# Last part of a decoder: the sums of the wide norm made on the activation engine, and the matrix engine a slot ahead

## The reference, cut to what matters

```python
h = layernorm(x, ln1_g, ln1_b)
h = bitlinear(h, w1, b1)                  # 256 -> 1024
h = jax.nn.gelu(h, approximate=False)
h = layernorm(h, ln2_g, ln2_b)            # over 1024 columns: "the wide norm"
h = bitlinear(h, w2, b2)                  # 1024 -> 256
x = _layernorm(x + h, axis=-1)
# bitlinear: x to integers in -128..127 by 127 / max|x| of the token, w to -1, 0, 1,
# the product, and both scales put back; layernorm: (x - mean) * rsqrt(var + 1e-5) * g + b
```

## Time and profile before

| | us |
|---|---|
| median of 3 runs | 2312.98 (2312.34 to 2318.16) |
| profiled execution | 2315.36 |
| its span | 2313.6 |
| last stage, from the first issue of a transfer to the end of the span | 2008.3 to 2313.6 |
| slot of the last stage (29 slots from the third `h` at 2032.46 to the last at 2291.71) | 8.94 |
| mean granted clock of TensorE over the span, as a share of full speed | 0.843 |

### The profile page before, as it was taken

How to read it: one execution, slowest core, us unless ns; L and a number is a source line. 1 busy time by engine, 2 the same in 40 slices (tenths; PEclk the granted TensorE clock), 3 DMA queues, 4 the chain that set the end, 5 groups by cost and what they waited for, 6 DMA issues and landing times. The chain is left out here.

```text
span 2313.6 us, 36269 instructions
## 1 busy us (share of the span) xinstructions
PE 1758.1 (76%) x12104; PEld 1097.3 (47%) x12104; DVE 1782.5 (77%) x4542; ACT 1333.4 (58%) x3347; POOL 847.5 (37%) x983
## 2 busy tenths in 40 slices
PE   8939999999968777775666666665899999556564
PEld 4503333333336566664444554434577667433333
DVE  4668888888626888885888888845578787599997
ACT  1204666666733344342078888899999992144443
POOL 2420000000007768753333333300575775323232
PEclk9957999999967989896777777767899999866766
DMA  2001111111020010000000000010000000000000
GB/s 79 19 21 29 30 30 30 30 28 29 12 63 15 12 31 13 12 6 19 1 19 1 1 1 1 1 35 23 1 19 1 1 1 1 30 12 16 14 15 18
DMA packets 42807, 41.54 MB, mean 18 GB/s; under 512 B 16054, under 2 KB 34670, under 8 KB 42622
## 3 DMA queue, kind: packets, MB, share of 16 engines
q1 hardware_dynamic: 42622, 39.23, 6.4%
HBM read 22.03 MB, written 4.19 MB: 11 GB/s over the span
## 5 line engine op out<-in xcount | busy, mean ns | idle before, releaser
L763 ACT ACTIVATE ST<-ST,aexp 128x1 f32<-128x1 f32 x2046 | 581.9, 384 | 2.0 <-PEq L57 2.0
L597 ACT ACTIVATE PT<-PS 128x512 f32<-128x512 f32 x576 | 309.8, 597 | 219.5 <-PE PS L482 188.6
L558 DVE CUSTOM_DVE_ANT_0 junk<-PS,maskw 128x128 bf16<-128x128 f32 (+3 forms) x512 | 226.5, 486 | 33.8 <-PE PS L459 33.8
L459 PE MATMUL PS<-KT,QT 48*128 48x512 bf16 (+3 forms) x768 | 190.1, 351 | 54.1 <-DMA QT<-QS 33.0
L561 DVE TENSOR_REDUCE MX<-PS 128x1 f32<-128x512 f32 x256 | 164.6, 685 | 27.7 <-PE PS L459 24.9
L501 PE MATMUL PS<-PT,VP 128*32 128x256 f32 (+1 forms) x2560 | 184.2, 370 | 0.0
L94 PE MATMUL PS<-ident,X 128*128 128x128 f32 x256 | 64.0, 339 | 143.7 <-DVE X L128 129.6
L631 POOL TENSOR_SCALAR nm<-MX 128x16 f32<-128x16 f32 x32 | 6.5, 203 | 431.1 <-DVE MX L564 431.1
L1663 PE MATMUL PS<-L_xattn_VW,l_pT 112*128 112x256 f32 x704 | 157.4, 379 | 2.9 <-issue 2.9
L459 PEld LDWEIGHTS PS<-KT,QT 48*128 48x128 bf16 x768 | 58.4, 94 | 200.0 <-issue 80.3
L1648 PE MATMUL PS<-Q,l_xT 128*128 128x512 f32 (+1 forms) x384 | 144.1, 526 | 1.7 <-DVE l_s L1696 1.7
(11 more groups left out here) (317 smaller groups left out, 4502.5 us busy)
## 6 DMA issues: line engine op xcount, KB each, us to landing
KT<-KS SPq DMA_DIRECT2D x192, 32.0 KB, 2.0
QT<-QS SPq DMA_DIRECT2D x192, 32.0 KB, 2.0
xs<-in_x SPq DMA_DIRECT2D x8, 512.0 KB
cx<-in_x SPq DMA_DIRECT2D x32, 128.0 KB, 2.0
out<-j_xn SPq DMA_DIRECT2D x32, 128.0 KB, 1.7
QT<-NMT SPq DMA_DIRECT2D x192, 2.0 KB
f_raw<-in_L_ffn_w SPq DMA_DIRECT2D x2, 1024.0 KB, 5.5
j_raw<-in_L_ffn_w SPq DMA_DIRECT2D x2, 1024.0 KB, 5.3
```

Source lines behind the costliest of these rows:

```text
L459: T.matmul(bank(u % 3)[:, 0:w * P], QT[i % R][rows, qt * P:(qt + 1) * P], KT[i % R][rows, k0 * P:(k0 + w) * P], start=True, stop=True).the ...
L558: V.tensor_tensor_reduce(junk[u % 3][:, 0:w * P], bank(u % 3)[:, 0:w * P], maskw[:, BANK - w * P:], 1.0, NEG, ALU.add, ALU.max, MX[i % 2][ ...
L597: C.activation(PT[n % 4][:, 2 * pr + e, 0:w], bank(3 + u % 3)[:, 0:w], ACT.Exp, scale=0.25).then_inc(e_done, 1)
L763: C.activation(self.ST[:, m, t:t + 1], self.ST[:, m, t - 1:t] if t else self.zero[:, :], ACT.Tanh, bias=self.BU[:, m, t:t + 1], scale=self ...
```

## The change

ACT gives sums as second outputs: Gelu also writes the sum of its 1024 results (`total`), a small multiplication on ACT makes it the negative mean (`nm`), and a new ACT pass, Square of (h + nm), writes the sum of the squares (`sq`) beside a result that nobody reads (`junk`). DVE's statistics and aggregate of the wide norm go away; one small DVE step makes variance plus epsilon (`ve`) from `sq`, POOL makes the power (`rs`), and the g pass takes `nm`.

The slots are laid anew. PE, with ACT's copy, is a slot ahead of DVE's `h`, which is now the first step of a DVE slot; the wide norm of a tile is made a slot after its Gelu and Square. In slot j DVE works on tile j-1 for `h`, on j-3 for the maximum, on j-2 for the wide norm and on j-4 for `y` and `xn`. PE does the second product before the next tile's transposes and first product, in its list. `y` and the moments of the last norm stand between the two passes. The four vectors are waited for one by one, the bias of `h` first, and DVE's `ds` is made without a wait.

```diff
         h, hn = [[store[:, (3 * m + u) * HID:(3 * m + u + 1) * HID] for u in range(3)] for m in range(2)]
         t2, hqT = ring(ctx, "j_t2", 2, [P, HID]), ring(ctx, "j_hqT", 2, [P, HID], BF16)
         y, xn = ring(ctx, "j_y", 2, [P, D]), ring(ctx, "j_xn", 4, [P, D])
-        vec_in, consts, j_xb, j_ds, j_tr, j_xqT, j_mm, j_h, j_gelu = st.sems("vec_in consts xb ds tr xqT mm h gelu")
+        total, nm, sq, ve, rs = (ring(ctx, f"j_{n}", 3, [P, 1]) for n in ("total", "nm", "sq", "ve", "rs"))
...
+        consts, j_xb, j_ds, j_tr, j_xqT, j_mm, j_h, j_gelu = st.sems("consts xb ds tr xqT mm h gelu")
+        bh_in, g2_in, b2_in, bo_in = vec_in = st.sems("bh_in g2_in b2_in bo_in")
...
+        j_nm, j_sq, j_ve, j_rs = st.sems("nm sq ve rs")
         out_st = st.slots("out_st", 4)
-        n2, n3, q2 = Norm(st, ctx, "n2", HID), Norm(st, ctx, "n3", D), Quant(st, ctx, "q2")
+        n3, q2 = Norm(st, ctx, "n3", D), Quant(st, ctx, "q2")
...
-            for d, n in ((g2_, "ln2_g"), (b2_, "ln2_b"), (bh, "b1"), (bo, "b2")):
-                SP.dma_start(d[:, :], row("L1_ffn_" + n)).then_inc(vec_in, 16)
+            for (d, n), landed_ in zip(((bh, "b1"), (g2_, "ln2_g"), (b2_, "ln2_b"), (bo, "b2")), vec_in):
+                SP.dma_start(d[:, :], row("L1_ffn_" + n)).then_inc(landed_, 16)
...
-            for j in range(NT + 2):
-                b, d = j, j - 2
+            for j in range(NT + 3):
+                a, d = j, j - 3
+                if on(a):
+                    if a >= 1:
+                        T.wait_ge(j_xqT, a)
+                    transposes(JQ[:, a, :], bank(0).bitcast(BF16), KD).then_inc(j_tr, 1)
+                    T.wait_ge(j_xqT, a + 1)
+                    if a >= 2:
+                        T.wait_ge(j_h, a - 1)
+                    for c in range(2):
+                        for k in range(KD):
+                            last = T.matmul(bank(1 + 2 * (a % 2) + c), xqT[a % 2][:, k * P:(k + 1) * P],
+                                            w1.wT[:, k, c * BANK:(c + 1) * BANK], start=k == 0, stop=k == KD - 1)
+                    last.then_inc(j_mm, 1)
                 if on(d):
                     T.wait_ge(j_t2, d + 1)
                     if d >= 1:
                         T.wait_ge(j_hqT, d)
                     transposes(t2[d % 2], bank(5, 2), KH).then_inc(j_hqtr, 1)
-                if on(b):
-                    if b >= 1:
-                        T.wait_ge(j_xqT, b)
-                    transposes(JQ[:, b, :], bank(0).bitcast(BF16), KD).then_inc(j_tr, 1)
-                if on(b):
-                    T.wait_ge(j_xqT, b + 1)
-                    if b >= 2:
-                        T.wait_ge(j_h, b - 1)
-                    for c in range(2):
-                        for k in range(KD):
-                            last = T.matmul(bank(1 + 2 * (b % 2) + c), xqT[b % 2][:, k * P:(k + 1) * P],
-                                            w1.wT[:, k, c * BANK:(c + 1) * BANK], start=k == 0, stop=k == KD - 1)
-                    last.then_inc(j_mm, 1)
-                if on(d):
                     T.wait_ge(j_hqT, d + 1)
                     if d >= 1:
                         T.wait_ge(n_y, d)
...
-            V.wait_ge(vec_in, 64)
...
-            for j in range(NT + 3):
-                b, c, d, e = j, j - 1, j - 2, j - 3
+            for j in range(NT + 4):
+                b, c, d, e = j - 1, j - 2, j - 3, j - 4
+                if on(b):
+                    if b == 0:
+                        V.wait_ge(bh_in, 16)
+                        V.wait_ge(j_ds, 1)
+                    V.wait_ge(j_mm, b + 1)
+                    V.scalar_tensor_tensor(h[b % 3][:, :], bank(1 + 2 * (b % 2), 2), ds[:, b:b + 1], bh[:, :], ALU.mult, ALU.add).then_inc(j_h, 1)
                 if on(d):
                     V.wait_ge(j_l2b, d + 1)
                     q2.dve_max(d, hn[d % 3][:, :])
                     q2.dve_level(d)
                     q2.dve_inverse(d)
                     V.tensor_scalar(ds2[d % 4][:, :], q2.amax[d % 4][:, :], w2.scale[:, :], None, ALU.mult).then_inc(j_ds2, 1)
+                if on(c):
+                    V.wait_ge(j_sq, c + 1)
+                    V.tensor_scalar(ve[c % 3][:, :], sq[c % 3][:, :], 1.0 / HID, EPS, ALU.mult, ALU.add).then_inc(j_ve, 1)
+                    if c == 0:
+                        V.wait_ge(g2_in, 16)
+                    if c >= 3:
+                        V.wait_ge(j_t2, c - 2)
+                    V.scalar_tensor_tensor(hn[c % 3][:, :], h[c % 3][:, :], nm[c % 3][:, :], g2_[:, :], ALU.add, ALU.mult).then_inc(j_l2g, 1)
                 if on(e):
                     V.wait_ge(j_mm2, e + 1)
                     V.wait_ge(j_xb, e + 1)
                     V.wait_ge(j_ds2, e + 1)
                     V.scalar_tensor_tensor(y[e % 2][:, :], bank(7)[:, 0:D], ds2[e % 4][:, :], xb[e % 6][:, :], ALU.mult, ALU.add).then_inc(n_y, 1)
-                if on(c):
-                    V.wait_ge(j_gelu, c + 1)
-                    n2.dve_stats(c, h[c % 3])
-                if on(e):
                     V.wait_ge(n_y, e + 1)
                     n3.dve_stats(e, y[e % 2])
-                if on(c):
-                    n2.dve_moments(c)
-                if on(e):
                     n3.dve_moments(e)
                 if on(c):
-                    if c >= 3:
-                        V.wait_ge(j_t2, c - 2)
-                    V.scalar_tensor_tensor(hn[c % 3][:, :], h[c % 3][:, :], n2.mv[c % 4][:, 0:1], g2_[:, :], ALU.subtract, ALU.mult).then_inc(j_l2g, 1)
+                    if c == 0:
+                        V.wait_ge(b2_in, 16)
+                    V.wait_ge(j_l2g, c + 1)
+                    V.wait_ge(j_rs, c + 1)
+                    V.scalar_tensor_tensor(hn[c % 3][:, :], hn[c % 3][:, :], rs[c % 3][:, :], b2_[:, :], ALU.mult, ALU.add).then_inc(j_l2b, 1)
                 if on(e):
                     if e >= 4:
                         V.wait_ge(out_st[e % 4], landed(e - 4, 4))
                     n3.dve_apply(e, xn[e % 4][:, :], y[e % 2][:, :]).then_inc(n_xn, 1)
-                if on(c):
-                    V.wait_ge(n2.rstd_done, c + 1)
-                    V.wait_ge(j_l2g, c + 1)
-                    V.scalar_tensor_tensor(hn[c % 3][:, :], hn[c % 3][:, :], n2.rs[c % 4][:, :], b2_[:, :], ALU.mult, ALU.add).then_inc(j_l2b, 1)
-                if on(b):
-                    V.wait_ge(j_mm, b + 1)
-                    V.wait_ge(j_ds, 1)
-                    V.scalar_tensor_tensor(h[b % 3][:, :], bank(1 + 2 * (b % 2), 2), ds[:, b:b + 1], bh[:, :], ALU.mult, ALU.add).then_inc(j_h, 1)
 
...
-            for j in range(NT + 2):
-                b, d = j, j - 2
+            for j in range(NT + 3):
+                a, b, c, d = j, j - 1, j - 2, j - 3
+                if on(a):
+                    C.wait_ge(j_tr, a + 1)
+                    if a >= 2:
+                        C.wait_ge(j_mm, a - 1)
+                    C.copy(xqT[a % 2][:, :], bank(0).bitcast(BF16)[:, 0:D]).then_inc(j_xqT, 1)
+                if on(b):
+                    C.wait_ge(j_h, b + 1)
+                    if b >= 3:
+                        C.wait_ge(j_l2g, b - 2)
+                    C.activation(h[b % 3][:, :], h[b % 3][:, :], ACT.Gelu, accum_out=total[b % 3][:, :]).then_inc(j_gelu, 1)
+                    C.wait_ge(j_gelu, b + 1)
+                    C.mul(nm[b % 3][:, :], total[b % 3][:, :], -1.0 / HID).then_inc(j_nm, 1)
                 if on(d):
                     C.wait_ge(q2.inv_done, d + 1)
                     if d >= 2:
...
                     C.activation(t2[d % 2][:, :], hn[d % 3][:, :], ACT.Identity, bias=up[:, :], scale=q2.qs[d % 4][:, :]).then_inc(j_t2, 1)
                 if on(b):
-                    C.wait_ge(j_tr, b + 1)
-                    if b >= 2:
-                        C.wait_ge(j_mm, b - 1)
-                    C.copy(xqT[b % 2][:, :], bank(0).bitcast(BF16)[:, 0:D]).then_inc(j_xqT, 1)
+                    C.wait_ge(j_nm, b + 1)
+                    if b >= 3:
+                        C.wait_ge(j_ve, b - 2)
+                    C.activation(junk[:, :], h[b % 3][:, :], ACT.Square, bias=nm[b % 3][:, :], scale=1.0, accum_out=sq[b % 3][:, :]).then_inc(j_sq, 1)
                 if on(d):
                     C.wait_ge(j_hqtr, d + 1)
                     if d >= 2:
                         C.wait_ge(j_mm2, d - 1)
                     C.activation(hqT[d % 2][:, :], bank(5, 2), ACT.Identity, bias=down[:, :], scale=1.0).then_inc(j_hqT, 1)
-                if on(b):
-                    C.wait_ge(j_h, b + 1)
-                    C.activation(h[b % 3][:, :], h[b % 3][:, :], ACT.Gelu).then_inc(j_gelu, 1)
 
         def pool():
-            G.wait_ge(vec_in, 64)
-            for j in range(NT + 3):
-                a, c, e = j, j - 1, j - 3
-                if on(c):
-                    n2.pool_rstd(c)
-                if on(e):
-                    n3.pool_rstd(e)
+            G.wait_ge(bo_in, 16)
+            for j in range(NT + 4):
+                a, c, e = j, j - 2, j - 4
```

(13 more changed lines are left out.)

## The result

The changed kernel takes 2274.31 us in the median of 4 runs (2272.22 to 2276.88), the kernel before 2314.54 beside it. The ratio is 0.9824 (95% interval 0.9811 to 0.9837): faster by 40 us. The forecast was 2276.5.

What follows compares the result with a forecast made beforehand. DVE bounds the kernel; the new slot lies between DVE's floor of 7.79 and an ACT-PE chain of 8.22 us, taken as 8.0. Span 2045.1 + 29 T = 2277.1, less 0.6: 2276.5 us, range 2267 to 2290.

Steps and rivals of the forecast that it cites:

- The bound: Last stage, full slots before the change: DVE sets the pace, busy 185.4 of 200 us, slots 8.94 us apart.
- DVE's list after the change: DVE's instructions in one new slot, added from start to start: 7.79 us, DVE's floor.
- The closed chain: ACT and PE, copy through Gelu, `t2`, second product to the next copy: 8.22 us at 1.2 GHz, 7.64 at mean clocks.
- The second output: ACT's sum written beside Gelu, a member of the closed chain: bounds 0 and 0.20 us, taken as 0.15.
- The slot of 8.0: Full slot of the last stage: between 7.79 and 8.22 us, middle taken; 2273 to 2280 us given 0.42.
- the floor: DVE's list in a new slot of the last stage: no slot under 7.79 us.
- the term T: Length of each of 29 full slots, 8.0 us, in the span 2045.1 + 29 T.
- DVE's floor rules: Rival for the full slots: T = 7.79, 2270.4 us; the floor or a little under it given 0.25.
- The stall that I had forecast ahead of `y`: DVE's wait in the full slots, ended by PE's second product, 7.7 us after Gelu's start.
- Start and end: Fill and drain of the last stage: first full slot at 2025.6, then 6.3 and 13.2 us; 9 us saved.
- The other rivals: ACT and clock: slow clock 0.22, dear outputs 0.06, slower (half-rate pass) 0.04, no change 0.01; table swaps given nothing.

Runs made afterwards that it cites:

- e7: Changed kernel's slot layout without the sums on ACT, DVE making the wide norm's statistics: 2322.2 us, 1.0022 of the kernel before.
- e5: Changed kernel plus an extra 1024-column ACT copy per slot between `nm` and `t2`, inside the closed chain: 2301.4 us, 0.9931 of the kernel before.
- e6: Changed kernel plus the same extra ACT copy behind the copy to `xqT`, outside the closed chain: 2275.8 us, 0.9825 of the kernel before.
- e11: Changed kernel with the extra copy between `nm` and `t2`, inputs turned a tile ahead and copied behind the Square: 2279.0 us, 0.9841 of the kernel before.
- e9: Changed kernel with the four vectors issued in the old order and one wait for all before `ds`: 2278.8 us, 0.9837 of the kernel before.
- e3: Changed kernel with `xn` moved behind the next slot's `h`: 2250.0 us, 0.9714 of the kernel before.
- e10: Changed kernel with `xn` behind the next `h`, inputs turned a tile ahead and copied behind the Square: 2248.0 us, 0.9707 of the kernel before.
- e8: Kernel before with Gelu's sum, `nm` and the Square behind `t2`, in the old slot layout: 2330.4 us, 1.0051 of the kernel before.

## Why the prediction came out as it did

**The bound.** Right: DVE's list is the slot before (8.94) and after, and without the sums too (9.35 in e7).

**DVE's list after the change, 7.79.** Right to the last digit, and its parts to 0.01: 2.81 to `ve`, 1.80 from the b pass to `xn`, and POOL's power for the b pass covered in the full slots.

**The closed chain.** Its length at 1.2 GHz was right (8.22 against 8.16), and so were its members; e5 and e6 show that it is one, e11 that it goes away when it is opened. The second output was taken at 0.15 and is an instruction of 0.189 that overlaps Gelu's end; Gelu to `nm` takes 1.18, not 1.25.

**The slot of 8.0: the step that was mis-sized.** I took the middle between the floor and the chain at 1.2 GHz, because I would not carry the mean clock over. As it came, the mean was 0.70 in both. That isn't a rule: e7, with the same order of PE's steps, had 0.54 over the same stretch. At 0.70, transposes 37.4/26.25 = 1.42 us and second product 43.1/26 = 1.66 make the chain 8.16 - 0.55 - 0.23 = 7.4 in the mean, under the floor, and the room ahead of `y` takes up the long ones; once it was used up (the slot of 7.87). What failed is thus the term T: 8.0 forecast, 7.79 measured, 6.1 us over 29 slots. The rival "DVE's floor rules" came true. The stall that I had forecast ahead of `y` stood in slot after slot only in e5.

**Why the time came out closer than T.** This was luck. The span was forecast at 2277.1 and was 2270.8. From the span I took off 0.6 for the median, as in the kernel before; in this one the median lies 3.5 above the profiled span. So the time misses by 2.2 us where the span misses by 6.3. The rival's span, 2271.0, was also met by terms that cancel: the stage began 1.0 earlier than before and its full slots 1.4 later within the stage, and the last two of the 29 were 0.3 shorter each.

**Start and end.** The first `h` came at 4.27 us after the first issue (4.2). The first full slot began at 18.7 and not at 17.3. POOL had three additions ahead of the first power, so the first b pass waited 1.23 us, 0.75 more than the 1.79 from pass to pass allow for; and the first two b passes took 1.63 and 1.68 instead of 1.28, each beside an addition of POOL. The single waits are worth 2.5 of the 7.9 us (e9); what the rest is made of (the shorter slots of fill and drain) was worked out, not tried apart. The slot behind the full ones was 6.28 (6.3); that the two ahead of it lack POOL's addition as well I had overlooked. From the last maximum to the end are 13.2, as before.

**The other rivals.** A pass with a sum isn't slower (1.058), the outputs aren't dear, and no table load stands in the slots: the trace has one for the stage, 1.28 us, ahead of the first Gelu. The Trainium skill, "ScalarE: Activation LUTs", section "Table sets: the hidden batching unit", doesn't name Square among the functions that every set has. In this kernel Gelu and Square alternate in every slot without a load between them, so Square runs with Gelu's set.

## What to carry to other kernels

Add up the list of the fullest engine from start to start, waits of the same form included; here that gave the new slot, 7.79 us, to 0.01. Then look for circles that the new order closes among the other engines, and give them their length at both clocks: one that is longer than the floor at 1.2 GHz can still be harmless (8.16 against 7.79 here), and one more instruction in it can cost almost its whole length (0.90 of 0.94 us a slot in e5). A mean clock of one variant is no basis for the next: here it was 0.54 to 0.84 for the same work and order of PE. Before reordering to open a circle, follow the products that the reordering makes late, since they may close another through the engine that was free.

## What the runs showed of the hardware

- ACT writes a sum as an instruction of its own, ACTIVATION_READ_ACCUMULATOR, 0.186 to 0.193 us in the mean, about twice DVE's 0.083; the pass itself isn't slowed, and the reader of the sum starts 1.18 us after a Gelu of 1.06.
- POOL and DVE slow each other. POOL's power of one column takes 1.52 us beside a DVE pass with two SBUF inputs (2022.75, the g pass) and 0.55 alone (2017.47); DVE's `xn` takes 0.73 beside POOL's addition and 0.41 without it.
- TensorE's mean granted clock, between 2060 and 2220 us, went with the slot and with the order of PE's steps, not with the slot alone. In the order of the changed kernel it was 0.55 at slots of 9.35 us (e7), 0.59 at 8.2 to 9.1 (e5), 0.67 to 0.72 at 7.79 (the changed kernel twice, e6, e9) and 0.84 at 6.87 (e3). With the input turned a tile ahead it was 0.65 at 7.79 (e11) and 0.74 at 6.87 (e10). In the order of before it was 0.68 at 9.45 (e8) and 0.70 at 8.94. In e7, the changed kernel and e3 DVE's list sets the slot, so there the shorter slot came first and the clock followed. Why the orders differ stays open.
